# Softmax scaling moved from VectorE to ScalarE, and VectorE's output reads put in another order, in a two-phase attention kernel

## What is computed

```
q  = rms_norm(x @ wq_a.T, q_norm_w) @ wq_b.T          # 32 heads of 128 + 64 rotary
kv = x @ wkv_a.T                                       # 128 latent + 64 rotary key
k_nope, v = split(rms_norm(kv[:, :128]) @ wkv_b.T)
scores = (q_nope . k_nope + q_pe . k_pe) * scale, causal
probs  = softmax(scores)
x = x + (probs . v) @ wo.T
```

## Time and profile before

| what | value |
|---|---|
| median of 3 runs | 2417.92 us (2414.95 to 2424.39) |
| the profiled execution's own time | 2421.19 us |
| its span, first to last instruction | 2419.6 us |
| TensorE busy | 2204.1 us (91%) |
| VectorE busy | 1888.5 us (78%) |
| ScalarE busy | 1161.4 us (48%) |
| GpSimd busy | 1281.6 us (53%) |
| mean granted TensorE clock | 0.983 of full |
| chain that ended last, by engine | PE 58%, DVE 20%, issue 9%, ACT 8%, DMA 2% |

### The profile page before, as it was taken

One profiled execution on the slowest core, in us unless ns is written; L12 is line 12 of the kernel. 1 busy time (PEld: TensorE's weight loads), 2 busy tenths in 40 slices (PEclk: granted clock), 3 DMA queues, 4 the chain that ended last, 5 costly groups with the idle time before them and its releaser, 6 DMA issues.

```text
span 2419.6 us, 44695 instructions
## 1 busy us (share of the span) xinstructions
PE 2204.1 (91%) x11548; PEld 1826.8 (76%) x11548; DVE 1888.5 (78%) x3912; ACT 1161.4 (48%) x3065; POOL 1281.6 (53%) x1658
## 2 busy tenths in 40 slices
PE   8988999888888999988889979999999999999988
PEld 7967777777777777777678967777777777777777
DVE  7667787778777877877887667888888888888887
ACT  6554545454445454454455544444444444444443
POOL 5346655656665556666545345555555555555543
PEclk9999999999999999999999999999999999999999
DMA  4023434433233344333334133333333333333321
GB/s 159 15 79 116 130 128 131 131 122 102 82 94 129 127 131 131 122 112 98 110 120 159 27 107 104 103 103 103 103 103 103 103 103 103 103 103 103 100 93 70
DMA packets 217104, 258.01 MB, mean 107 GB/s; under 512 B 145616, under 2 KB 174416, under 8 KB 214992
## 3 DMA queue, kind: packets, MB, share of 16 engines
q1 hardware_dynamic: 212432, 244.64, 32.6%
q10 hardware_dynamic: 4608, 12.58, 1.5%
HBM read 127.14 MB, written 79.69 MB: 85 GB/s over the span
## 4 chain that ended last, share of the span: by engine, by line
PE 58%; DVE 20%; issue 9%; ACT 8%; DMA 2%; POOL 1%; SPq 1%; DVEq 0%; ACTq 0%; POOLq 0%
PE ps L835 44%; DVE stage L2136 6%; DVE xacc L2151 5%; PE ps L914 4%; ACT arena L1353 4%; PE ps L1194 3%; DVE arena L1798 3%; PE ps L1138 2%; DVE negmax L2126 2%; ACT stage L1353 1%; PE ps L861 1%; DVE ps L2124 1%; ACT stage L1650 1%; DVE ps L2117 1%; PE ps L849 1%
## 5 line engine op out<-in xcount | busy, mean ns | idle before, releaser
L835 PE MATMUL ps<-arena,extra 128*128 128x512 f32 x1920 | 549.1, 416 | 137.5 <-DVE xacc L2151 137.2
L2151 DVE TENSOR_TENSOR xacc<-ps,xacc 128x512 f32<-128x512 f32 x896 | 590.8, 682 | 86.4 <-PE ps L835 72.9
L1798 DVE TENSOR_TENSOR arena<-ps,arena 128x512 fp32r<-128x512 f32 (+4 forms) x728 | 418.0, 576 | 294.7 <-ACT arena L1353 294.3
L835 PEld LDWEIGHTS ps<-arena,extra 128*128 128x128 f32 x1920 | 343.9, 192 | 247.0 <-DVE xacc L2151 170.9
L1650 ACT ACTIVATE stage<-ps,negmax 128x128 f32<-128x128 f32 (+6 forms) x512 | 260.3, 508 | 467.3 <-DVE negmax L2126 464.2
L835 PE MATMUL ps<-zT,arena 128*128 128x512 f32 (+1 forms) x1746 | 453.7, 404 | 17.0 <-POOL arena L2389 8.6
L1353 ACT ACTIVATE arena<-ps 128x512 fp32r<-128x512 f32 (+4 forms) x728 | 365.7, 505 | 196.6 <-PE ps L835 87.1
L835 PEld LDWEIGHTS ps<-zT,arena 128*128 128x128 f32 x1746 | 314.3, 190 | 82.4 <-issue 10.9
L2433 POOL TENSOR_TENSOR extra_plain<-extra_plain,arena_plain 128x128 f32<-128x128 f32 x128 | 66.0, 515 | 452.8 <-ACT extra_plain L1353 452.8
L2136 DVE TENSOR_SCALAR stage<-stage,rrec 128x128 f32<-128x128 f32 (+6 forms) x512 | 301.4, 650 | 4.5
L835 PE MATMUL ps<-keyT,arena 128*128 128x192 f32 (+5 forms) x1152 | 267.3, 340 | 18.3 <-ACT stage L1650 18.3
(11 more groups left out here) (129 smaller groups left out, 3266.9 us busy)
## 6 DMA issues: line engine op xcount, KB each, us to landing
kept_b<-arena SPq DMA_DIRECT2D x16, 3584.0 KB, 11.0
arena<-kept_b SPq DMA_DIRECT2D x112, 512.0 KB, 4.8
arena<-arena SPq DMA_DIRECT2D x128, 128.0 KB, 3.0
stage<-in_wo SPq DMA_DIRECT2D x16, 1024.0 KB, 13.0
stage<-stage SPq DMA_DIRECT2D x248, 64.0 KB, 2.0
extra<-arena SPq DMA_DIRECT2D x120, 128.0 KB, 3.0
kept_q<-arena SPq DMA_DIRECT2D x16, 768.0 KB, 4.8
arena<-kept_q ACTq DMA_DIRECT2D x32, 384.0 KB, 3.8
```

What stands on the lines that cost most here:

```text
L835: last = nc.tensor.matmul(dst, w, m, start=start and n == 0, stop=stop and n == len(passes) - 1, skip_group_check=skip)
L1798: return nc.vector.tensor_tensor(dst, src, part.bitcast(F32), ALU.subtract)
L2151: nc.vector.tensor_tensor(xs, bank_y(k, j), xs, ALU.add).then_inc(y_added, 1)
```

## The change

ScalarE gets a function `norms`, which waits for VectorE's reciprocals and multiplies the four blocks by them with a Copy activation whose scale is a per-partition operand. VectorE's `norms` becomes `inverses`, the reciprocal alone. In VectorE's slot the output read 0 moves ahead of `pt_split` 2, read 4 ahead of the "first" fill, and the split of B22 in slot 2 of pair 0 behind the inverses.

```diff
@@ scalar, first_body (four such places)
                 exps(p, 0, 1, 1)
+                norms(p, 0, 0)
                 turn(0, 0)
@@ scalar
+            def norms(p, g, k):
+                n, u = slot_n(p, g, k), k % 2
+                act.wait_ge(rec_ready, n + 1)
+                for i in range(NS):
+                    pr = prob[u][:, poff(u, i):poff(u, i) + keys_of(u, i)]
+                    nc.scalar.activation(pr, pr, ACT.Copy, scale=rrec[:, u, i:i + 1]).then_inc(prob_ready, 1)
@@ scalar, body
                     exps(p, g, k, 3)
                     turned(n, before, 3)
+                    norms(p, g, k)
                     if k == 1 and p == 0:
                         split_b(g, T1, last)
@@ vector
-            def norms(p, g, k):
+            def inverses(p, g, k):
                 n, u = slot_n(p, g, k), k % 2
                 dve.wait_ge(exp_done, 4 * n + NS)
                 nc.vector.reciprocal(rrec[:, u, :], rowsum[:, u, :]).then_inc(rec_ready, 1)
-                dve.wait_ge(rec_ready, n + 1)
-                for i in range(NS):
-                    pr = prob[u][:, poff(u, i):poff(u, i) + keys_of(u, i)]
-                    nc.vector.tensor_scalar(pr, pr, rrec[:, u, i:i + 1], None, ALU.mult).then_inc(prob_ready, 1)
@@ vector, slot
                 maxima(p, g, k, 2)
+                adds(0)
                 pt_split(n, before, 2)
-                adds(0, 1)
+                adds(1)
                 fills("second")
                 maxima(p, g, k, 3)
+                adds(2, 3)
+                pt_split(n, before, 3)
+                inverses(p, g, k)
                 if k == 2 and p == 0:
                     split_b(g, B22)
-                adds(2, 3)
-                pt_split(n, before, 3)
-                norms(p, g, k)
                 if early:
                     mom_early(g, k)
+                adds(4)
                 fills("first")
-                adds(4, 5)
+                adds(5)
```

More of the change, by code:

```diff
@@ L1541, in first_body @@
                 valued(slot_n(p, 0, 0))
+                norms(p, 0, 1)
                 fills("q2")
@@ L1573, in first_body @@
                 exps(p, 0, 2, 3)
+                norms(p, 0, 2)
                 if p == 0:
@@ L1590, in first_body @@
                 turn(2, 3)
+                norms(p, 0, 3)
                 fills("q1")
@@ L2031, in first_body @@
                 maxi(1, 1)
-                norms(p, 0, 0)
+                inverses(p, 0, 0)
                 turn(0, 0)
@@ L2039, in first_body @@
                 maxi(1, 3)
-                norms(p, 0, 1)
+                inverses(p, 0, 1)
                 turn(1, 0)
@@ L2062, in first_body @@
                     adds(2, 0, 1)
-                    norms(p, 0, 2)
+                    inverses(p, 0, 2)
                     split_b(0, T3)
@@ L2093, in first_body @@
                 turn(2, 3)
-                norms(p, 0, 3)
+                inverses(p, 0, 3)
                 fills("q1")
```

## The result

The kernel before takes 2419.86 us (median of 4 runs beside the changed one), the changed kernel 2355.06 us (2349.76 to 2363.93, 4 runs). The ratio is 0.973, 95% interval [0.971, 0.9751]: 65 us less, where 79 were forecast; the range from 2298 to 2386 us holds it. The profiled execution took 2349.76 us, span 2348.1, against 2419.6 before: 71.5 us less.

The account below looks back on a forecast made before the run. TensorE, 91% busy, was taken as the bound, but not alone: it mostly waits for VectorE's output reads. Savings of 29 us (pair 1), 47 (pair 0) and 3 (first groups, drains) sum to 79, giving 2339 us; range 2298 to 2386.

Parts of the forecast that it names:

- The narrow slot: Pair 1: output 2 starts earlier, output 6 without a gap; the slot takes 13.6 us, 1.9 to 2.0 less.
- The wide slot, POOL next: Pair 1: ScalarE waits 1.3 to 1.4 us for POOL's last sum; the slot grows to 15.4 or 15.5 us.
- The rival that POOL's chain doesn't bind: Wide slots stay at 14.54 us; 57 us saved in pair 1, 55 in pair 0, 2303 us; chance 0.22.
- Pair 0: Per body, slot 0 gains 1.0 us, slot 2 2.65 (slot 1's 0.2 included), slot 3 loses 0.5: 3.15, fifteen times 47.
- the prediction's own sign: Wrong if TensorE's scores wait over 0.3 us for a query fill's low part, meaning ScalarE binds.
- its other sign: Wrong if the stretch at clock 0.70 in pair 0's slot 2 stays.
- the 0.70 stretch: Pair 0, slot 2: clock 0.70 over 5.67 us behind the 2.80 us stall, expected to go, worth 1.7 us.
- The copies: ScalarE's four scaled copies hold its queue about 2.25 us in wide and 1.45 us in narrow slots.
- The first groups and the two drains: Outside the counted bodies: a few of these stalls each, 3 us of gain put for all.
- The slower rival: ScalarE's wide copies delay the fill read and next scores in 60 wide slots; 2468 us at double length; chance 0.05.
- its break-even: Wide four copies 1.4 us over 2.25, so 3.65 us, eat the 79 us gain.
- 2.80 gives 0.70, 1.36 gives 1.00: Pair 0: the clock was 0.70 behind a 2.80 us stall, but stayed at 1.00 with one of 1.36 us.

Follow-up runs that it names:

- late split: The changed kernel with ScalarE's second split in wide slots moved behind `turned` 2: 2320.90 us, ratio 0.9569 to the kernel before.
- Order alone: The changed kernel's new VectorE order with the multiplications left on VectorE: 2380.19 us, ratio 0.9811 to the kernel before.

## Why the prediction was right, and where it wasn't

- **The narrow slot.** Forecast 13.6 to 13.7, measured 13.62 us. Output 2 waits for nothing, output 3's weight load waits 0.52 us (0.35 forecast), output 6 has no gap.
- **The wide slot, POOL next.** Forecast 15.4 to 15.5, measured 15.50; ScalarE's wait forecast at 1.3 to 1.4, measured 1.34; output 2's 0.6 measured as 0.46. Two slots 29.12 for 29.2, and 27.6 us over 29 pairs for the 29 us forecast over 30. The late split shows the cause. The rival that POOL's chain doesn't bind is refuted, and its price was good in pair 1: with the chain out of the way two slots take 28.19, and 1.9 x 30 = 57 us were named for it, against 30.08 - 28.19 = 1.89. Its price for pair 0 (55 us) was not: there the late split gives 2 us more than the change (957.3 for 959.4).
- **Pair 0.** Forecast 47 us, measured 47.5 over 29 half bodies, and that close a match is partly luck. A typical body takes 68.8 us before and 65.9 after: the first 13 bodies save 37.0 us, 2.85 each against the 3.15 forecast. The last body and a half save 10.4. They are not like the others, though the text ahead of the prediction has "one body stands for all": VectorE also runs `mom_early` in the last two, and the first of them takes 74.1 us before, at a mean clock of 0.93, and 67.9 after, at 0.97. By slots in a typical body: slot 0 14.48 us for 15.62 (1.14 less, 1.0 forecast), slots 1 and 2 together 2.48 less (2.65), slot 3 0.76 more (0.5). Output 3 waits 1.30 us (1.4). Within the sum one wait was missed: slot 2's first scores wait 0.59 us for the low part of fill q3, which was seen as late but not as awaited, and output 0 waits 0.86 us for POOL where 0.4 was put. By the prediction's own sign (over 0.3 us of waiting for such a low part) ScalarE's list binds here, and its other sign, a slow stretch that stays, holds in five of 13 bodies.
- **The clock in pair 0: a term with the wrong mechanism.** The prediction priced the end of the 0.70 stretch at 1.7 us, from one body; by its own count 1.05 us of slot 2's 2.65 lie behind output 3. Three of the first 13 bodies before the change keep the clock at 1.00 through slot 2, behind a stall as long, and the slot takes 19.37 us there, against 19.35 in the earlier trace rows:

```profile
577.88 1.75 PE L835 MATMUL ps<-arena,extra 128*128 128x512 f32 x6 [2.78 <-DVE xacc L2151]
...
585.87 0.97 PE L835 MATMUL ps<-arena,extra 128*128 128x512 f32 x3 [1.23 <-DVE xacc L2151]
...
567.30:586.67 19.37, 14.40 (x79) 11.64 (x78) 15.91 (x30) 8.72 (x24) 16.15 (x18) 1.00 0.06 14
```

  At full speed TensorE reaches output 6 sooner and waits 1.23 us there for `y_add` 4, behind the multiplications; in the body of the earlier trace rows, at half speed, it does not wait. In 8 of the 10 bodies with a slow stretch it cost nothing (19.35 to 19.44 us), in two 1.3 us (20.64 and 20.68). So the clock's return was worth 0.2 us a body on the mean of these 13; what paid is `y_add` 4 no longer standing behind the multiplications, which the prediction did not see in slot 2. The sum was nearly right, this part of its working was not.
- **The copies.** Forecast 2.25 us for the wide four and 1.45 for the narrow, measured 2.25 and 1.44. ScalarE's gain was put at 280 us and is 218: single durations were added up, with the overlap of 0.1 us counted in each, while the page counts overlapped time once. The copies by element count:

```profile
L1663 ACT ACTIVATE stage<-stage,rrec 128x512 f32<-128x512 f32 x64 | 45.3, 708 | 0.0
L1663 ACT ACTIVATE stage<-stage,rrec 128x128 f32<-128x128 f32 x128 | 44.5, 395 | 55.4 <-DVE rrec L2144 55.4
```

  So 708 ns at 512 and 395 at 128: the plain copies' 628 and 306 and some 80 to 90 more, close to the 93 ns that the exponential showed.
- **The step that failed**: "The first groups and the two drains have a few of these stalls each; I put 3 us for all." It was a guess by likeness, with no row behind it. Pair 0's first group lost 4.8 us in its second half, and pair 1's 2.6. In pair 0 ScalarE sits for 4.02 us behind VectorE's reciprocals, with the read of fill pe0 behind that wait; before, the read stood right behind the exponentials. Pair 1's loss, 2.3 of it in the first half, comes with the copies: that half takes 23.4 to 24.0 us in the four kernels with the multiplications on VectorE and 26.0 to 28.7 in the eight with them on ScalarE. TensorE's wait for a low part there grows from 1.10 to 2.16 us; the chain behind it was not followed. The forecast was 79 us and the spans show 71.5; these two groups are 7.4 of loss where 3 of gain were put, which the other stretches in part made up. The medians give 65 us; the profiled execution of the changed kernel is the fastest of its four.
- **The slower rival** was the right one to name: 1.5 us more on ScalarE in wide slots turns the gain into a loss of 1.1%. Its price held (92 us more than the changed kernel for 1.5 us in 60 slots); its break-even, 3.65 us for the four, was too high, since it rested on a gain of 79 us. By the two measured points, 92 us for 1.55 us added, the gain of 65 is gone at 1.1 us more, so at about 3.3 to 3.4 us for the four; that is an estimate.
- **What the prediction did not say**: that in pair 1 the move of the multiplications is worth nothing beside the new order, and that in pair 0 neither part is worth much without the other. Its sum was made over the whole change and never split by part.

The page "SBUF — State Buffer" of the Trainium skill, section "SBUF: two separate sides", says that ScalarE never waits on another engine at its ports. The trace agrees: ScalarE's narrow four take 1.44 or 1.45 us in all 53 narrow slots looked at, with POOL's rotation running beside them, where VectorE's took 3.05. POOL gains less than the earlier trace rows let one expect: in pair 1 its second rotation step takes at most 1.31 us in all 26 narrow slots looked at, where 13 of 25 took 1.36 to 1.38 before; in slot 2 of pair 0 it takes 1.53 us, starting while VectorE's split of B22 still runs. That the split is the cause is not shown.

The rule of "ScalarE: Activation LUTs" that the prediction cites from the Trainium skill gives its "up to about" three times for bf16. These operands are fp32, and the wide four take 1.5 times as long on ScalarE (2.25 us against 1.48).

## What to carry to other kernels

Where engines run fixed lists joined by semaphores, work is not moved to an idle engine but into its list: ask what stands behind the new entry, and what waits for that. The same four copies, in wide slots, cost or gave 50 us by standing ahead of or behind one read. And after removing a stall look for the chain that did not move with it, here one that starts from a DMA: a wait in one position of the next engine's list turned 55 us of gain in pair 1 into 28, and moving one instruction gave it back; in pair 0, where a transfer of weights came next, it gave almost nothing. Last, read more than one body: a slow clock ahead of a wait for another engine can cost nothing, and a last body can carry work that the others don't.

## What was not expected of the hardware

The clock does not follow from a stall's length. Order alone, two bodies of pair 0 have the same two stalls in slot 2 (1.49 and 2.09 us, 1.47 and 2.09), and the granted clock behind the second differs. Windows behind output 3 of the one body, then of the other:

```profile
714.21:717.00 2.79, 2.79 (x17) 2.48 (x18) 2.43 (x6) 1.66 (x4) 2.02 (x3) 1.00 0.30 71
717.00:720.00 3.00, 3.00 (x15) 2.37 (x13) 2.96 (x6) 0.00 (x0) 2.64 (x3) 1.00 0.00 0
...
723.00:726.00 3.00, 3.00 (x13) 2.91 (x12) 1.59 (x4) 0.62 (x3) 2.05 (x4) 0.50 0.64 108
783.08:786.00 2.92, 2.92 (x14) 2.65 (x15) 2.51 (x7) 1.26 (x4) 2.12 (x3) 0.72 0.29 67
786.00:789.00 3.00, 3.00 (x11) 2.38 (x10) 3.00 (x5) 0.39 (x1) 2.64 (x3) 0.71 0.00 0
```

In the first body the clock held full speed (2.4 GHz) for 5.8 us and fell to half (1.2 GHz) only behind the further stall of 1.89 us at 721.95; in the second it was partly at half at once. The prediction took "2.80 gives 0.70, 1.36 gives 1.00" from two stalls. Neither half holds in every body. Before the change a stall of 2.78 us has 1.00 behind it in three of 13 bodies (577.88, above). In the changed kernel the clock falls in slot 2 of five of 13, with nothing longer than 1.3 us of idle time ahead of it; in one of them the six matmuls of outputs 0 and 1 take 2.56 us, where they took 1.64 at 696.11:

```profile
562.13 0.58 PE L835 MATMUL ps<-keyT,arena 128*128 128x192 f32 x3 [1.27 <-ACT stage L1654]
...
564.23 2.56 PE L835 MATMUL ps<-arena 128*128 128x512 f32 x6 [0.86 <-POOL arena L2439]
...
557.14:574.85 17.71, 15.58 (x78) 12.82 (x79) 14.16 (x27) 9.59 (x28) 15.79 (x16) 0.90 0.06 15
```

This slot too is as long as one at full speed (17.71 against 17.73 us), since it then no longer waits at output 3. In a wide slot, where TensorE is the bound, the same fall costs time: with the order alone slot 3 of most bodies of pair 0 takes 15.2 us, and 16.6 to 16.8 in the five of 13 in which the clock falls. What decides when it falls was not tried.
